# The inverse inside a gated delta rule: two doublings on a compact form, with products of a quarter of the array

## The reference, cut to what matters

```
def step(S, inp):
    q_t, k_t, v_t, g_t, b_t = inp
    S = S * jnp.exp(g_t)[..., None, None]
    mem = jnp.einsum('bhk,bhkv->bhv', k_t, S)
    delta = (v_t - mem) * b_t[..., None]
    S = S + jnp.einsum('bhk,bhv->bhkv', k_t, delta)
    o_t = jnp.einsum('bhk,bhkv->bhv', q_t * scale, S)
    return (S, o_t)
```

## Time and profile before

| | |
|---|---|
| time, median of 3 runs | 5456.53 us (5451.6 to 5461.41) |
| span of the profiled execution, which is its own time | 5452.6 us |
| busy in it: TensorE, VectorE, ScalarE, GpSimd | 89%, 70%, 50%, 42% |
| chunks of the first layer | 32, from about 130 to 2690 us |
| granted TensorE clock, mean over the span | 0.926 of full speed |

### The profile page before, as it was taken

The page is one execution under the profiler, slowest core; times in us unless marked ns, Lnnn a source line. Parts: engine busy times, 40 slices in busy tenths (PEclk is TensorE's granted clock), DMA queues, the critical chain, the costliest instruction groups (busy, mean ns, idle before and its releaser), DMA issues. The chain is left out here.

```text
span 5452.6 us, 104905 instructions
## 1 busy us (share of the span) xinstructions
PE 4831.1 (89%) x36890; PEld 3535.1 (65%) x36890; DVE 3836.5 (70%) x9111; ACT 2736.9 (50%) x6711; POOL 2285.8 (42%) x1860
## 2 busy tenths in 40 slices
PE   5999999999999999999889989984488778998998
PEld 3787777877777787777766556641156665654665
DVE  4766667777677766767578668746699657866874
ACT  2444445444544544545478658724400116875882
POOL 2434334344334434434267347514322116743751
PEclk7999999999999999999999999986699758998998
DMA  2000000000000000000100000000000000000000
GB/s 86 5 9 7 7 9 7 7 9 7 7 9 10 5 9 8 6 9 9 34 1 0 25 5 0 0 7 0 8 1 1 1 1 30 0 24 5 0 0 16
DMA packets 170085, 52.60 MB, mean 10 GB/s; under 512 B 142304, under 2 KB 166112, under 8 KB 168928
## 3 DMA queue, kind: packets, MB, share of 16 engines
q1 hardware_dynamic: 168160, 44.30, 3.7%
q10 hardware_dynamic: 1536, 3.21, 0.2%
HBM read 36.99 MB, written 10.49 MB: 9 GB/s over the span
## 5 line engine op out<-in xcount | busy, mean ns | idle before, releaser
L799 DVE SCALAR_TENSOR_TENSOR gd_qkT<-gd_ps,gd_w_qk,gd_qkT 128x256 f32<-128x256 f32 x768 | 367.2, 482 | 193.3 <-ACT gd_qkT L632 172.7
L984 POOL TENSOR_TENSOR gd_gV<-gd_g,cst 128x512 f32<-128x512 f32 x128 | 130.3, 1040 | 860.1 <-PE gd_ps L510 860.1
L417 PE MATMUL gd_ps<-gd_taps,gd_xwins 128*128 128x512 f32 x1024 | 465.3, 597 | 0.0
L676 ACT ACTIVATE gd_X<-gd_ps 128x512 f32<-128x512 f32 x384 | 201.1, 620 | 452.9 <-PE gd_ps L496 452.6
L1540 ACT ACTIVATE L_ffn_s<-L_ffn_s,L_ffn_nb,L_ffn_r 128x128 f32<-128x128 f32 x1024 | 419.4, 482 | 3.1
L1360 POOL TENSOR_TENSOR L_ffn_t<-L_ffn_t 128x512 f32<-128x512 f32 x128 | 190.2, 1486 | 391.8 <-DVE L_ffn_t L1581 391.8
L417 PEld LDWEIGHTS gd_ps<-gd_taps,gd_xwins 128*128 128x128 f32 x1024 | 192.8, 191 | 191.1 <-issue 185.6
L868 DVE TENSOR_TENSOR gd_Z<-gd_ps,cst 128x256 f32<-128x256 f32 x384 | 162.7, 424 | 129.6 <-PE gd_ps L512 111.1
L1579 DVE TENSOR_TENSOR L_ffn_t<-L_ffn_ps,L_ffn_sb_rope 128x512 f32<-128x512 f32 x256 | 176.8, 691 | 101.8 <-PE L_ffn_ps L1385 101.8
L521 PE MATMUL gd_ps<-gd_Z,gd_X 128*128 128x64 f32 x2048 | 239.2, 275 | 0.0
L512 PE MATMUL gd_ps<-gd_gV,gd_nA 128*128 128x64 f32 x2048 | 237.9, 275 | 0.0
(11 more groups left out here) (389 smaller groups left out, 13625.6 us busy)
## 6 DMA issues: line engine op xcount, KB each, us to landing
L_ffn_sb_rope<-in_rope SPq DMA_DIRECT2D x4, 2048.0 KB, 8.3
gd_tap_row<-in_L_attn_conv_v SPq DMA_DIRECT2D x2, 2048.0 KB, 15.6
gd_blocks<-gd_nA SPq DMA_DIRECT2D x256, 16.0 KB, 1.7
gd_Z<-gd_blocks SPq DMA_DIRECT2D x32, 128.0 KB, 2.0
gd_inverses<-gd_Z SPq DMA_DIRECT2D x32, 128.0 KB, 1.7
gd_gV<-gd_inverses SPq DMA_DIRECT2D x256, 16.0 KB, 1.9
L_ffn_sb_wqkv<-in_L_ffn_wqkv SPq DMA_DIRECT2D x4, 768.0 KB, 8.9
out<-out_tok SPq DMA_DIRECT2D x8, 256.0 KB, 2.6
```

Source lines behind the costliest of these rows:

```text
L417: ins = pe.matmul(ps[4 + i % 2][:], xwin(j)[:, t:t + P], taps[:, t, 512 * i:512 * (i + 1)], start=(t == 0), stop=(t == TAPS - 1))
L676: act.activation(heads(X, gi).rearrange("p h x -> p (h x)"), ps[4 + gi][:], ACT.Copy).then_inc(x_s.sem, 1)
L799: ins = dve.scalar_tensor_tensor(produced(j, i), ps[6 + i % 2][:, P + t:P + t + WIDE], w_tap[:, at, t:t + 1], produced(j, i), ALU.mult, AL ...
```

## The change

The two doublings of 16 and 32 stay within halves of 64 rows. So the small inverses now go into a compact `Tc` of 64 columns for a head (the lower half's blocks stand beside the upper half's), and both doublings work on `Tc`:

- turn (`half_turn`): a transpose takes two heads at once, 8 transposes for 16 heads and not 16.
- z and tz (`half_z`, `half_tz`): each product has 64x64 weights, a quarter of the array, and 32 moving columns, 32 products for all heads in each step. They stand in an order that goes around the four quarters. The first product of each step has weights of 64x128.
- There is one group of 16 heads: one mask (`mask_z`) of 128x512 for all, and one addition (`merge16`, and for 32 two of 64x512, `merge32`), and not four each.

After the second doubling the full `Tm` is made: `merge32` writes the even blocks of 32, and GpSimd the odd ones by an operation of 128x1024 that multiplies by a mask (`odd_s`). The doubling of 64 has 64x64 weights (before: 128x64), and its z products of groups 2 and 3 alternate with the tz products of groups 0 and 1; `last_z` of VectorE is now a plain copy. VectorE's two parts of the decays go ahead of the residues, and the residues are spread. GpSimd clears `Tc` in addition to `Tm`. The eight PSUM banks are one tensor.

```diff
@@ -17,13 +17,13 @@
-LEVELS = [16, 32, 64]
+LEVELS = [16, 32]
...
@@ -192,7 +192,8 @@
-        ps = [ctx.enter_context(nc.psum_tensor(f"gd_ps{i}", [P, 512], F32)) for i in range(8)]
+        banks = ctx.enter_context(nc.psum_tensor("gd_ps", [P, 8, 512], F32))
+        ps = [banks[:, i] for i in range(8)]
...
@@ -264,8 +265,10 @@
-        Tm, R = gV, v
+        Tm, Tc, R = gV, sb("Tc", [P, H, HALF]), v
         PT, yT, y, squares = decay, X, delta, X
+        Xc = X[:, 0:H // 2]
+        Zc = Z[:].rearrange("p h x -> p (h x)")[:, 0:2 * 8 * 32].rearrange("p (r k x) -> p r k x", r=2, k=H // 2)
...
@@ -372,10 +385,10 @@
-                    sp.wait_ge(*Tm_zero.now(n))
+                    sp.wait_ge(*Tc_zero.now(n))
                     sp.wait_ge(*inv_out.now(n))
                     for q in range(NB):
-                        sp.dma_start(diagonal(Tm, q), inverse_dram[q].rearrange("h i j -> i h j")).then_inc(T_in.sem, 16)
+                        sp.dma_start(Tc[BASE * q:BASE * (q + 1), :, BASE * (q % 4):BASE * (q % 4 + 1)], inverse_dram[q].rearrange("h i j -> i h j")).then_inc(T_in.sem, 16)
...
@@ -491,41 +504,82 @@
+                def half_turn(n, l):
+                    for i in range(2):
+                        if l:
+                            w(T16_s.now(n))
+                        else:
+                            w(o1_s.now(n, 2 + i))
+                        for k in range(4):
+                            h = 8 * i + 2 * k
+                            ins = pe.transpose(ps[6 + i][:, P * k:P * (k + 1)], Tc[:, h:h + 2].rearrange("p h x -> p (h x)"), ident)
+                        ins.then_inc(xc_mm.sem, 1)
+
+                def half_z(n, l):
+                    for k in range(H // 2):
+                        for r in range(2):
+                            for c in range(2):
+                                h = 2 * k + c
+                                part = slice(0, P) if k == r == c == 0 else None
+                                ins = pe.matmul(banks[part or rows(c), 4 + r, 32 * k:32 * (k + 1)], nA[rows(r), h, part or rows(r)],
+                                                even(Tc, h, h + 1, LEVELS[l])[rows(r), 0], start=True, stop=True)
+                    ins.then_inc(zc_mm.sem, 1)
+
+                def half_tz(n, l):
+                    w(xc_s.now(n, 2 * l + 1)); w(zc_s.now(n, l))
+                    for k in range(H // 2):
+                        for c in range(2):
+                            for r in range(2):
+                                part = slice(0, P) if k == r == c == 0 else rows(r)
+                                ins = pe.matmul(banks[part, 4 + c, 32 * k:32 * (k + 1)], Xc[rows(c), k, part],
+                                                Zc[rows(c), r, k], start=True, stop=True)
+                    ins.then_inc(tzc_mm.sem, 1)
+
                 def turn_T(n, gi):
+                    w(odd_s.now(n)); w(T32_s.now(n))
                     for k in range(HG):
-                        ins = pe.transpose(ps[4 + gi][:, P * k:P * (k + 1)], Tm[:, HG * gi + k], ident)
+                        ins = pe.transpose(ps[(6, 7, 4, 5)[gi]][:, P * k:P * (k + 1)], Tm[:, HG * gi + k], ident)
                     ins.then_inc(x_mm.sem, 1)
+
+                def last_z(n, gi, k):
+                    h = HG * gi + k
+                    part = slice(HALF if k else 0, P)
+                    return pe.matmul(ps[gi][part, 64 * k:64 * (k + 1)], nA[0:HALF, h, part], Tm[0:HALF, h, 0:HALF], start=True, stop=True)
+
+                def last_tz(n, gi, k):
+                    h = HG * gi + k
+                    n = 1 if k else 2
+                    return pe.matmul(ps[gi][0:HALF * n, 64 * k:64 * (k + 1)], Z[HALF:P, h:h + n].rearrange("p h x -> p (h x)"), X[HALF:P, h, HALF:P], start=True, stop=True)
 
                 def solve(n):
                     w(T_in.now(n))
+                    for l in range(len(LEVELS)):
+                        half_turn(n, l)
+                        half_z(n, l)
+                        half_tz(n, l)
+                    for gi in range(2):
+                        turn_T(n, gi)
+                    for gi in range(2):
+                        w(R_s.now(n, gi))
+                        for k in range(HG):
+                            ins = last_z(n, gi, k)
+                        ins.then_inc(z_mm.sem, 1)
+                    for gi in range(2, G):
+                        turn_T(n, gi)
+                    for gi in range(2, G):
+                        w(R_s.now(n, gi)); w(z_s.now(n, gi - 2)); w(x_s.now(n, gi - 2))
+                        for k in range(HG):
+                            first = last_z(n, gi, k)
+                            second = last_tz(n, gi - 2, k)
+                        first.then_inc(z_mm.sem, 1)
+                        second.then_inc(tz_mm.sem, 1)
+                    for gi in range(2, G):
+                        w(z_s.now(n, gi)); w(x_s.now(n, gi))
+                        for k in range(HG):
+                            ins = last_tz(n, gi, k)
+                        ins.then_inc(tz_mm.sem, 1)
                     for gi in range(G):
-                        w(o1_s.now(n, gi))
-                        turn_T(n, gi)
-                    for l, s in enumerate(LEVELS):
-                        for gi in range(G):
-                            w(Tl_s.now(n, G * (l - 1) + gi) if l else R_s.now(n, gi))
-                            for k in range(HG):
-                                h = HG * gi + k
-                                if s == HALF:
-                                    ins = pe.matmul(ps[gi][HALF:P, 64 * k:64 * (k + 1)], nA[:, h, HALF:P], Tm[:, h, 0:HALF], start=True, stop=True)
-                                else:
-                                    ins = pe.matmul(ps[gi][:, 64 * k:64 * (k + 1)], nA[:, h], even(Tm, h, h + 1, s)[:, 0], start=True, stop=True)
-                            ins.then_inc(z_mm.sem, 1)
-                        for gi in range(G):
-                            w(z_s.now(n, G * l + gi)); w(x_s.now(n, G * l + gi))
-                            for k in range(HG):
-                                h = HG * gi + k
-                                if s == HALF:
-                                    ins = pe.matmul(ps[gi][0:HALF, 64 * k:64 * (k + 1)], Z[:, h], X[:, h, HALF:P], start=True, stop=True)
-                                else:
-                                    ins = pe.matmul(ps[gi][:, 64 * k:64 * (k + 1)], X[:, h], Z[:, h], start=True, stop=True)
-                            ins.then_inc(tz_mm.sem, 1)
-                        if s < HALF:
-                            for gi in range(G):
-                                w(Tl_s.now(n, G * l + gi))
-                                turn_T(n, gi)
-                    for gi in range(G):
-                        w(Tl_s.now(n, G * (NL - 1) + gi))
+                        w(T64_s.now(n, gi))
...
@@ -670,10 +724,13 @@
-                    for l in range(NL):
-                        for gi in range(G):
-                            w(x_mm.now(n, G * l + gi))
-                            act.activation(heads(X, gi).rearrange("p h x -> p (h x)"), ps[4 + gi][:], ACT.Copy).then_inc(x_s.sem, 1)
+                    for l in range(len(LEVELS)):
+                        for i in range(2):
+                            w(xc_mm.now(n, 2 * l + i))
+                            act.activation(Xc[:, 4 * i:4 * (i + 1)].rearrange("p h x -> p (h x)"), ps[6 + i], ACT.Copy).then_inc(xc_s.sem, 1)
+                    for gi in range(G):
+                        w(x_mm.now(n, gi))
+                        act.activation(heads(X, gi).rearrange("p h x -> p (h x)"), ps[(6, 7, 4, 5)[gi]], ACT.Copy).then_inc(x_s.sem, 1)
...
@@ -851,29 +908,41 @@
-                def level(n, l):
-                    s = LEVELS[l]
-                    for gi in range(G):
-                        w(z_mm.now(n, G * l + gi))
-                        mask = cst[:, C_MERGE + 64 * l:C_MERGE + 64 * (l + 1)].unsqueeze(1).to_broadcast([P, HG, 64])
-                        dve.tensor_tensor(heads(Z, gi), ps[gi][:, 0:256].rearrange("p (h x) -> p h x", h=HG), mask, ALU.mult).then_inc(z_s.sem, 1)
-                    for gi in range(G):
-                        w(tz_mm.now(n, G * l + gi))
-                        te = even(Tm, HG * gi, HG * (gi + 1), s)
-                        if s == HALF:
-                            dve.tensor_copy(heads(X, gi)[0:HALF, :, HALF:P],
-                                            ps[gi][0:HALF, 0:256].rearrange("p (h x) -> p h x", h=HG)).then_inc(Tl_s.sem, 1)
-                        else:
-                            dve.tensor_tensor(te, ps[gi][:, 0:256].rearrange("p (h n s) -> p h n s", h=HG, s=s), te, ALU.add).then_inc(Tl_s.sem, 1)
+                def residues(n, gi):
+                    if gi == 0:
+                        w(nec_s.now(n))
+                    w(ks_mm.now(n, gi)); w(vn_s.now(n, gi))
+                    for k in range(HG):
```

(65 more changed lines are left out.)

19 lines of the change are left out of this document (6 added, 13 removed).

## The result

The changed kernel takes 5655.61 us (median of 4 runs, 5643.67 to 5676.84), the kernel before 5455.88 us beside it: ratio 1.036, 95% interval 1.033 to 1.039, about 200 us slower. The forecast was 5687.

A forecast was written before the change was run, and what follows sets the result against it. TensorE's 23.3 us stretch in each of 32 chunks was taken as the bound. 20.4 + 8.1 + 2.0 = 30.5 us, 7.2 more a chunk, +230 us: 5687 us, range 5500 to 5790; slower 0.81.

The forecast's parts named there:

- The clock: TensorE's clock falls about 4.5 us into the rewritten stretch: 8.1 us there plus 2.0 in deltas and outputs; chance 0.68.
- the first rival: Dense work around the compact levels keeps the clock up, the 20.4 us stretch stands: 5364 us, chance 0.13.
- The stretch at the upper clock: TensorE from first turn to deltas, each chunk: 20.4 us against 23.3 at 2.4 GHz.
- turns, with the wait for ScalarE: 32 transposes instead of 48 in the stretch, 3.6 us a chunk, plus 0.35 average wait for the state products.
- four narrow steps, start to end of the last: z and tz of the two compact levels: 64 matmuls a step, 1.8 us each, 7.2 us against 14.2.
- VectorE's stops: TensorE waits after the narrow steps for masks and additions, formerly hidden: 3.7 us a chunk.
- 64 matmuls of the last level: Doubling of 64 on quarters, with six changes of form at about 0.45 us: 5.5 us against 3.7.
- Clock holds: Same as the first rival: upper clock throughout the stretch, 5364 us (5310 to 5440), chance 0.13.
- slow narrow products: Clock holds but narrow products of the compact levels cost 0.045 us each: 5505 us, chance 0.07.
- falls in part: Clock falls only in part of the chunks, or late in the last level: half the price, 5575 us, chance 0.12.
- odd blocks: GpSimd's 128x1024 operation after `merge16`: 2.1 us, wanted over 6 us later, so hidden even at twice that.
- later wait for `o1_s`: First turn waits for the third state product on ScalarE, not the first: 0.7 us every second chunk, 0.35 average.

The follow-up runs named there:

- short_fill_last_new: short_fill with the changed kernel's level of 64 (64x64 and 64x128 weights): 5366.73 us, ratio 0.984 to the kernel before.
- short_fill: Changed kernel with the old level of 64 and one unread product (128x128 weights, 512 columns) in each of four TensorE stops: 5302.56 us, repeated 5300.26.
- odd_twice: short_fill with GpSimd's operation for the odd blocks done twice, one after the other: 5297.21 us, ratio 0.969 to the kernel before.
- last_old: Changed kernel with only the level of 64 put back in its earlier form: 5439.15 us, ratio 0.996 to the kernel before.
- narrow_fill_22: short_fill with 22 unread products (64x64 weights, 32 columns, around four quarters) in each stop instead of the full one: 5372.04 us, ratio 0.983.
- before_last_new: Kernel before with only the level of 64 in the changed kernel's forms (64x64 weights, first head of a group 64x128): 5648.74 us, ratio 1.037.
- full_in_step: last_old with three unread 512-column products inside each of the four narrow steps, the stops left empty: 5678.53 us, ratio 1.040.
- quarter_fill: short_fill with its unread products on a quarter of the array (64x64 weights, 480 columns, plus 32 under 64x128): 5340.13 us, ratio 0.979.

## Why the prediction was right

**The clock.** The fall came 5.1 us after the first turn; I took 4.5. Low to the deltas and 4.3 us into them (2.0 us lost; 2.0 forecast). With the clock held, short_fill_last_new has a stretch of 19.97 us (1154.56 to 1174.53); less 0.09 us for each of three fillers it is 19.7, so the low clock costs 28.0 - 19.7 = 8.3 us of stretch (8.1 forecast). That the two lie so close is partly luck. The forecast was 12.5 us of TensorE's work at 1.65 times its length; by an estimate from these rows it was 11.3 us (the 22.9 us at the lower clock, less the 3.3 of stops in them, less 8.3) at 1.73 times. Its time of 5367 is near the 5364 of the first rival, which is the other side of the same sum. The changed kernel is 289 us slower than it, with the same products and without the fillers: this shows that the clock, and no other wait, makes the change a loss.

**The stretch at the upper clock.** 20.4 forecast, 19.7 measured, out of terms that err in both directions:

| term, us a chunk | forecast | measured |
|---|---|---|
| turns, with the wait for ScalarE | 3.95 (3.6 + 0.35) | 4.5 (1.53 + 0.97 + 0.99 + 1.03) |
| four narrow steps, start to end of the last | 7.2 | 5.8 (4 x 1.46) |
| VectorE's stops | 3.7 | 4.2 (0.90, 0.80, 0.90, 1.61) |
| 64 matmuls of the last level | 5.5 | 5.1 (1.70 + 1.57 + 1.85) |

The narrow steps lie near their lower bound. In short_fill's first one, behind the wide product, this row stands for 57 of the 64 matmuls:

```profile
1134.78 1.04 PE L528 MATMUL gd_ps<-gd_Tc,gd_nA 64*64 64x32 f32 x57
```

The last of them takes 0.22 us, so the 56 steps between starts are 0.82 us, 0.015 each, the lower bound of 0.014 and not the 0.02 that I took. So the 25 ns of the Trainium skill (TensorE: Matmul & The Clock Gate, Part 1) is no floor across four quarters; the trace disagrees with it. In the last level the forecast's terms were right in kind: 0.058 a matmul on one quarter (0.056 forecast), 0.029 alternating (0.03), and six changes of form at 0.39 us (0.45). The 0.4 us too much lie in the changes of form.

**The size.** 5687 against 5656: the chunk was forecast 7.2 us longer, this chunk is 28.0 - 23.3 + 2.0 = 6.7, the mean 6.3.

**Rivals.** "Clock holds" (5364), "slow narrow products" (5505) and "falls in part" (5575) did not happen. The odd blocks are hidden, as odd_twice shows; for the second clearing no run tests it. The later wait for `o1_s`: I put it at 0.35 us a chunk. In the 31 chunks of the changed kernel the wait of the first turns for ScalarE was

```profile
PE gd_ps L515 <- ACT gd_o L725: 18.4, 38, 0.7
PE gd_ps L515 <- DMA gd_Tc<-gd_inverses: 12.8, 10, 2.4
```

0.6 us a chunk, and that for the DMAs 0.4, where it was about 0.9 (26.5 us for 16 waits, before). So it mostly took the place of a DMA wait.

**What it did not see.** I treated the stretch as one cause. The last level's new form is half of the low time and, in time, more than the whole loss: last_old against the changed kernel is 216 us, and with the old form there the two compact levels gain 18 us even with their low time of 16 us. But the parts do not add up: with fillers in the compact levels the same form costs only 64 us. As products the quarter forms save nothing in this level: a matmul of 64 columns under 64 rows takes as long as under 128, and the changes of form come on top.

**Open.** What the clock follows is not settled. Busy time is excluded (narrow_fill_22, before_last_new), stops of 0.8 to 1.6 us alone are (full_in_step), and the working part of the array as the only measure is (quarter_fill). Few columns in a matmul do not explain it alone either: the level of 64 in the kernel before has 64 columns too, and its clock holds. before_last_new changed two things there, the quarter weights and the eight changes of form; no run has the quarter weights without a wide product in each group, which would part the two. Whether that form is faster by itself is untested too. Longer waits play a part as well: in short_fill the only low time inside the stretch followed waits of 2.4 and 2.7 us for the DMAs.

## What to carry to other kernels

Where a stretch of small products stands in a chain, read the granted clock of that stretch before counting its instructions: 10 us of low clock (8.3 in the stretch, 2.0 in the deltas) outweighed 3.6 us of saved work a chunk. If the clock falls there, one product that nothing reads, put into a stop that exists anyway, can be worth more than the whole rewrite (5656 to 5367, and 5300 with the old last level). And quarter weights pay only where neighbours in the row sit on other quarters, and where the form of the weights changes seldom.

## What I had not expected of the hardware

A float32 matmul under weights of 64 columns starts 0.058 us after the one before it on the same place, whether the weights have 128 rows (short_fill, L552) or 64 (short_fill_last_new, L553), and under 128x128 weights it is 0.11. So halving the rows gained nothing. Halving the moving columns gained nothing on one quarter either: around four quarters with 32 columns it is 4 x 0.015 us until the same quarter is used again. What pays is that the quarters overlap. And a wide product among quarter products costs 0.39 us each time, nearly as much as seven matmuls on one quarter.
